# A fused two-layer transformer tower: late moments and roots moved, activations ahead of three stages, two first loads held back

## The reference

```python
h = _L0_tok_ref(x, L0_tok_W)                       # embedding and position table
h = h + _L0_attn_ref(_layernorm(h, axis=-1), ...)  # 8 heads, softmax, out-projection, own layer norm
h = h + _L0_ffn_ref(_layernorm(h, axis=-1), ...)   # per batch 2 of 8 experts: gelu(gelu(x w1 + b1) w2 + b2)
h = h + _L1_attn_ref(_layernorm(h, axis=-1), ...)  # token i of a block attends over blocks, softmax, projection
h = h + _L1_ffn_ref(_layernorm(h, axis=-1), ...)   # per token 2 of 8 experts: gelu(x W1 + b1) W2 + b2
```

## Time and profile before

| | before |
|---|---|
| median of 3 runs | 1405.86 us (1405.33 to 1407.46) |
| profiled execution | 1408.95 us |
| its span | 1407.1 us |
| TensorE matmul busy | 1187.5 us (84%) |
| ScalarE busy | 995.0 us (71%) |
| VectorE busy | 934.7 us (66%) |
| GpSimd busy | 564.4 us (40%) |
| first score of first attention | 55.78 us |
| first turn of the first experts | 631.74 us |
| first turn of second attention | 857.48 us |
| first turn of the second experts | 1094.99 us |

### The profile page before, as it was taken

One profiled execution on the slowest core, in us unless ns is written; L12 is line 12 of the kernel. 1 busy time (PEld: TensorE's weight loads), 2 busy tenths in 40 slices (PEclk: granted clock), 3 DMA queues, 4 the chain that ended last, 5 costly groups with the idle time before them and its releaser, 6 DMA issues. The chain is left out here.

```text
span 1407.1 us, 26982 instructions
## 1 busy us (share of the span) xinstructions
PE 1187.5 (84%) x9386; PEld 795.1 (57%) x9386; DVE 934.7 (66%) x2612; ACT 995.0 (71%) x1348; POOL 564.4 (40%) x546
## 2 busy tenths in 40 slices
PE   3599999999999999889989996888872899999940
PEld 2244444444444444447768874777762688888830
DVE  4255868686868686758978884677662466666625
ACT  0288888888888888858868984454520799999930
POOL 3413333333333333210201000077777177777660
PEclk9599999999999999979999997889875899999975
DMA  3655565555555555223211300011115577777609
GB/s 86 119 129 146 120 157 130 147 130 148 139 138 137 138 135 139 84 71 124 88 61 61 119 2 8 1 49 47 50 47 174 181 242 237 241 245 244 234 24 358
DMA packets 93163, 180.57 MB, mean 128 GB/s; under 512 B 15597, under 2 KB 64200, under 8 KB 84960
## 3 DMA queue, kind: packets, MB, share of 16 engines
q1 hardware_dynamic: 72832, 129.18, 32.8%
q0 software_dynamic: 17344, 42.68, 9.4%
q10 hardware_dynamic: 2848, 6.95, 1.7%
HBM read 116.96 MB, written 63.12 MB: 128 GB/s over the span
## 5 line engine op out<-in xcount | busy, mean ns | idle before, releaser
L741 ACT ACTIVATE a_probs<-a_psS 128x1024 f32<-128x1024 f32 x512 | 484.0, 1034 | 91.5 <-PE a_psS L826 58.2
L838 PE MATMUL a_psO<-a_probs,a_v 128*32 128x256 f32 x4096 | 282.1, 394 | 17.3 <-DVE a_o_t L1015 16.9
L1252 DVE TENSOR_TENSOR f_g_lo<-f_g,f_g_hi 128x512 fp32r<-128x512 f32 x284 | 195.1, 689 | 121.1 <-ACT f_g L1159 120.1
L2044 POOL DMA_INDIRECT result<-f_out,f_idx x156 | 182.7, 1171 | 92.5 <-issue 61.0
L838 PEld LDWEIGHTS a_psO<-a_probs,a_v 128*32 128x32 f32 x4096 | 108.5, 111 | 154.0 <-issue 88.9
L1636 POOL DMA_INDIRECT queue<-all_row,all_idx x128 | 126.0, 984 | 38.5 <-issue 37.8
L826 PE MATMUL a_psS<-ag_qs,ag_ks 50*128 50x512 f32 x512 | 97.4, 457 | 15.7 <-DMA ag_qs<-a_gparts 8.5
L826 PE MATMUL a_psS<-a_qs,a_ks 50*128 50x512 f32 x512 | 96.8, 454 | 7.8 <-issue 3.4
L402 POOL TENSOR_TENSOR ag_rs_f<-ag_veps_f,all_half 128x4 f32<-128x4 f32 x32 | 34.1, 1066 | 124.4 <-DVE ag_veps_f L99 124.4
L1422 POOL TENSOR_TENSOR ah_rs<-ah_veps,all_half 128x4 f32<-128x4 f32 x16 | 18.5, 1156 | 154.3 <-DVE ah_veps L1435 154.2
L826 PEld LDWEIGHTS a_psS<-ag_qs,ag_ks 50*128 50x128 f32 x512 | 39.9, 191 | 63.4 <-issue 31.6
(11 more groups left out here) (368 smaller groups left out, 2878.8 us busy)
## 6 DMA issues: line engine op xcount, KB each, us to landing
all_w<-experts SPq DMA_DIRECT2D x19, 1026.5 KB, 5.5
experts<-a_split POOLq DMA_DIRECT2D x32, 512.0 KB, 4.8
ag_qs<-experts SPq DMA_DIRECT2D x14, 1026.5 KB, 5.3
ag_ks<-experts SPq DMA_DIRECT2D x14, 1026.5 KB, 5.2
all_rows<-queue SPq DMA_DIRECT2D x39, 260.0 KB, 5.1
f_w<-experts SPq DMA_DIRECT2D x8, 1026.5 KB, 5.5
qparts<-a_parts SPq DMA_DIRECT2D x16, 512.0 KB, 4.5
kparts<-a_parts SPq DMA_DIRECT2D x14, 512.0 KB, 3.1
```

Source lines behind the costliest of these rows:

```text
L741: nc.scalar.activation(probs[u % NPR][:, :], psS[score_buffer(u)][:, :, :].rearrange("p a n -> p (a n)"), ACT.Exp).then_inc(exp_done, 1)
L838: last = nc.tensor.matmul(psO[32 * g:32 * g + 32, a * HALF:(a + 1) * HALF], v[par][:, 2 * hp + p, kt, :], probs[u % NPR][:, cols:cols + HA ...
L1252: nc.vector.tensor_tensor(g_lo[i][:, n, :], g[:, n, :], g_hi[i][:, n, :].bitcast(F32), ALU.subtract).then_inc(lo_done, 1)
L2044: pool.indirect_dma_start(result, bass.IndirectOffsetOnAxis(ap=idx[i][:, j:j + 1], axis=0), out[i][:, j, :], None, bounds_check=2 * B * S ...
```

## The change

Four edits.

1. **First batch's second loads.** SyncE stores the second half of the queries, then waits for the guard (`wait_guard`), then loads the second halves of both queries and keys. ScalarE only stores the second half of the keys and no longer loads it.
2. **Gelu ahead.** `expert_items` gets a tile of one column, and ScalarE begins its list there with a gelu of a column of `ident` into it. This holds for both experts' blocks; in the first one ScalarE's four transfers still come before.
3. **Exponential ahead.** In second attention ScalarE begins with an exponential of one column of `half`.
4. **Last moments and roots.** `close` is gone; its work becomes `last_moments`, which VectorE runs in second attention between the split of the first batch's rows and the wait for `cleared`. GpSimd runs the last two of the 16 roots in second attention, between its clearing of the counts and the first root of that stage.

```diff
@@ block.sync of embed_and_attend
             redistribute(sp, 0, 0, 0, 0)
-            redistribute(sp, 0, 0, 0, 1)
+            store_parts(sp, 0, 0, 1)
+            wait_guard(sp, 0)
+            load_parts(sp, 0, 0, 0, 1)
+            load_parts(sp, 0, 0, 1, 1)
             sp.wait_ge(cleared, 4)
@@ block.scalar of embed_and_attend
-            for ch in range(CPB):
-                redistribute(act, 0, 0, 1, ch)
+            redistribute(act, 0, 0, 1, 0)
+            store_parts(act, 0, 1, 1)
             rounds(batch)
@@ expert_items
+    warm = c.sb("warm", [P, 1])
@@ block.scalar of expert_items
+        nc.scalar.activation(warm[:, :], ident[:, 0:1], ACT.Gelu)
         first_bits(0)
@@ block.vector of expert_items
         back(N - 1)
-        if aside is not None:
-            aside.close(dve)
@@ Rest
-    def close(self, dve):
-        last = self.ahead.B * self.ahead.T // TPC - 1
-        self.ahead.spread(dve, last - 1)
-        dve.drain()
-        self.ahead.sums(dve, last, self.H)
-        self.ahead.spread(dve, last)
@@ Ahead
+    def last_moments(self, dve, H):
+        j = self.B * self.T // TPC - 1
+        self.spread(dve, j - 1)
+        self.sums(dve, j, H)
+        self.spread(dve, j)
@@ block.gpsimd of sequence_experts
-            for j in range(5, B * CPB):
+            for j in range(5, B * CPB - 2):
                 ahead.root(pool, j)
@@ block.gpsimd of block_attention
             pool.sem_inc(cleared, 1)
+            for j in (B * CPB - 2, B * CPB - 1):
+                ahead.root(pool, j)
             for b in range(B):
@@ block.scalar of block_attention
+            nc.scalar.activation(warm[:, :], half[:, 0:1], ACT.Exp)
             for ch in range(CPB):
                 places(0, ch)
@@ block.vector of block_attention
             split_x(0)
+            ahead.last_moments(dve, H)
             dve.wait_ge(cleared, 1)
```

## The result

| | before | after |
|---|---|---|
| median | 1405.46 us (20 runs) | 1398.0 us (20 runs) |
| ratio | | 0.9945 [0.993, 0.9961] |
| profiled execution | 1408.95 us | 1399.67 us |
| its span | 1407.1 us | 1397.9 us |

The change makes the kernel 7.7 us faster (5.5 to 9.8, the ratio against 1405.46). Forecast were 10.95 us and 1394.9, with a range of 1389.5 to 1400. The direction and the range held; the gain was forecast 3 us too large, above the interval.

A forecast was written before the change was run, and what follows sets the result against it. Bounds: five stalls at stage starts and ends, with GpSimd's fixed-pitch sends pacing second attention and second experts. Sum 5.9 - 0.3 + 3.5 + 0.95 + 0.9 = 10.95 us; 1405.86 - 10.95 = 1394.9 us, range 1389.5 to 1400.

The forecast's parts named there:

- guard: First batch of first attention: with second loads held back, the guard lands at 49.8 instead of 55.67; gain 5.9 us (3.4 to 6.2).
- first experts, gelu ahead: Start of first experts: table load and one-column gelu delay the first product; cost 0.3 us, bounds +0.2 and +1.5.
- moments and roots: End of first experts: second attention starts 0.35 us after the last weighing, at 853.96; gain 3.5 us.
- second attention, exponential ahead: Second attention: everything starts 0.35 us later, the exponential follows its copy 1.30 us earlier; net gain 0.95 us (0.7 to 1.3).
- second experts, gelu ahead: Second experts: load hidden in ScalarE's wait; 0.9 of 1.28 us reach TensorE and the first result sent, bounds 0 and 1.3.
- late by itself: Rival, first batch: GpSimd's own start delays the guard, so holding loads gains nothing; 5.05 us left, 1400.8; chance 0.12.
- The cover of the held loads: First batch: held key loads land by 61.5 plus one us, first read after 79; cost nothing, 16 us of cover.
- either sending stage gets longer: Sign of being wrong, second attention and second experts: first-to-last send distance was to stay unchanged in both.
- The clock rises sooner: Rival, first batch: TensorE's clock rises at once after the shorter pause, saving 5.2 us more; 1389.7; chance 0.10.
- a rise at another distance than 16 us from the first score: Sign of being wrong, first batch: TensorE's clock was to rise 16 us from the first score.
- Table not kept: Rival, second attention and both experts: copies between need another table, so each load comes back; 7.55 us gain, 1398.3; chance 0.04.
- clock stays down: Slower rival, first batch: TensorE's clock no longer rises near 72, each exponential costs 0.49 us more; 1420.9; chance 0.03.

## Why the prediction was right, and where it was not

| term, us gained | forecast | first pair of profiles | executions with it against those without |
|---|---|---|---|
| guard | 5.9 | 7.16 | 3.9 to 4.5 |
| first experts, gelu ahead | -0.3 | -1.15 to item 4 | -0.15 to -1.15 to item 4; -0.8 to -1.8 to the end, new tile included |
| moments and roots | 3.5 | 3.55 | 3.55 |
| second attention, exponential ahead | 0.95 | 2.28 to the first exponential | 1.0 or 2.1 to the first exponential; 1.9 to 3.1 to the end |
| second experts, gelu ahead | 0.9 | 0.25 | 0.25 |

To the end, for the first experts, is from turn to last weighing: 223.37 to 224.35 us with gelu and tile against 222.53 to 222.59 in three kernels without (221.87 in the profile of before). For second attention it is from its turn to that of the second experts: 234.4 to 235.1 against 237.1 to 237.5. With middle values, 4.2 for the guard, -1.5 for the first experts and 2.6 for second attention, the right column gives 4.2 - 1.5 + 3.55 + 2.6 + 0.25 = 9.1 us, inside both intervals of the whole (5.5 to 9.8, and 5.9 to 13.6 where the changed kernel ran again).

- **Guard.** The mechanism was right and the rival "late by itself" wrong: alone it landed in 2.2 us. The size failed at the step that took 9.4 us from the earlier trace rows as what is removed. That was one execution's bad draw; others had 6.4 and 6.8. The step that took 3.5 us as the new landing erred the other way, by 1.3, and hid part of it; so the first score, at 48.62, came before the 49.5 to 52.3 of the forecast and the landing before its 3 to 6 us. The Trainium skill's estimate from "DMA: Bandwidth & Descriptors", section "Anatomy of one DMA", 2.04 us, agrees with the 2.1 to 2.3 measured; its section "Queues, rings and completion order", taken to mean that a small transfer gets its turn soon among large ones, does not describe this place, where four query loads were enough to make it 4.5 to 6.4.
- **The cover of the held loads.** It was enough: the first batch was no longer for it (67.3 to 68.5 us with and without, apart from the two with the late rise of the clock), and the landings of 6.7 to 9.1 us end by 61, before the 79 of the forecast.
- **First experts.** The shift of the first product (1.37 us, against 1.48) was forecast, and its cost put between 0.2 and 1.5. The step that failed was to take TensorE's idle 0.9 us from 640 to 650, where the clock stood at 1.00, as room for it: the time is lost before, while TensorE is at 0.50 and the bound. The 0.5 us or so that the new tile takes from this stage were not in the sum at all.
- **Moments.** Right to 0.05 us; the moved work ended at 859.00, 3 us before VectorE went on with the scores at 862.04.
- **Second attention.** Forecast 0.95. To the first exponential and at like clock it is that: the first exponential came 14.32 and 14.47 us behind the turn where the clock rose at 10.4 and 10.8, against 15.25 to 15.60 without it, where it rose at 9.9 to 10.1. In the six other profiles with it in this place the clock rose 7.5 to 7.8 us behind the turn and the exponential came after 13.32 to 13.35. Whether the earlier rise is the change's or chance is open. It hardly matters: the stage as a whole was 1.9 to 3.1 us shorter in all eight, the two with the late rise included (234.85 and 234.38). The step that failed was to take the first exponential's shift for that of the first send and of the stage's end: the first send came 54.5 to 55.5 us behind the turn, against 57.0 to 57.2 without. Where the later work gains the rest is not settled.
- **Second experts.** The first gelu did come 1.27 us sooner and the first result sent 0.93 (23.98 us behind the turn instead of 24.91), as forecast. The step from there to the end failed: the sends were to keep their distance, and took 0.67 us more. That is the new tile, a cost that the sum did not have at all. The prediction's own sign for it ("either sending stage gets longer") showed.
- **The clock rises sooner.** In the first pair of profiles it looked as if this rival had come true (4.12 us in the first batch). The prediction's sign of being wrong, a rise at another distance than 16 us from the first score, showed too, at 7.1. But it is not the change's work: kernels without the held loads have 7.3, and with half of them held 7.6. The profile of before was the odd one, and the 16 us were read from it alone.
- **Table not kept, clock stays down.** Neither came true: there is one table load per stage, kept even over a stage's end.

What of the 9.28 us between the profiles is the change and what is chance could not have been read from that pair. That the range held owes something to luck: too much for the guard and too little for second attention nearly cancel. What the new tile costs the first experts lies for the most part between items 12 and 16, which took 34.7 to 35.0 us in the eight executions with it and 33.5 to 34.5 in the six without, two of these with a gelu table loaded ahead. TensorE's clock falls to 0.50 there in each; why the stretch is longer with the tile is not settled.

## What to carry to other kernels

A stall that ends with a DMA's landing has a price only over several executions: here one profile's 9.4 us was 6.4 to 6.8 in others, so take the spread over executions for the gain, and not the one value on the page. Read a gain at the end of its stage too: the exponential ahead gave 1.0 or 2.1 us at the first exponential, by the clock, and some 2.6 at the stage's end either way. A table load that is moved ahead is free where the engine waits anyway, but it delays whatever stands behind it on that engine, and if TensorE is at its lower clock at that point, most of the delay can count (up to 1.15 of 1.37 us here). Write a throw-away output into a tile that is there: a new one shifts those behind it, and that alone can cost nearly as much as the edit gains (0.67 us against 0.93 in the second experts).

## What the runs showed of the hardware that had not been expected

- Large loads beside them made four small transfers take 4.8 us at the median with four loads, and 4.1, 4.5 and 6.8 with eight, instead of 2.2.
- Two profiles of the same kernel differed by 15.8 us (1397.9 and 1382.1) with the same instructions, 12.8 us of it in the first attention, where VectorE and ScalarE were equally busy and TensorE's clock was not the same: drops to 0.50 behind pauses of 1.3 us, 1.45 us each, which hit from none to five of six batches, and a low stretch behind a pause in the eighth batch. Over all executions of the table that batch took 67.6 to 78.2 us.
- A tile of 4 or 64 bytes a partition, written once in the stage, made the sends of a stage, 245.0 us, take 0.7 to 0.8 us longer. Since writing into a tile that exists does not, it should be where the tiles behind it came to lie; that was not tested apart.
